# Mask rows inside the key and query tiles of two attentions, a transposed layout for squares, and a copy moved to GpSimd

## What is computed

```
# second: x = layernorm(h)
qkv = x @ qkv_w + qkv_b;  q, k = layernorm(q)*w+b, layernorm(k)*w+b   # over 64
o = softmax(q*scale @ k.T) @ v;  o = gates * o;   h += o @ proj_w + proj_b
# third: x = layernorm(h)
q, k, v = x @ qkv_w.T, in 12 heads of 64
q = q * rsqrt(norm(q, over the 12 heads) + 1e-8);  k likewise
o = softmax(q @ k.T / scale[head]) @ v;   h += o @ w_out.T + b_out
```

## Time and profile before

| | us |
|---|---|
| median of 3 runs | 1608.81 (1606.82 to 1610.09) |
| the profiled execution, its own time | 1603.52 |
| its span, first to last instruction | 1601.7 |

### The profile page before, as it was taken

How to read it: one execution, slowest core, us unless ns; L and a number is a source line. 1 busy time by engine, 2 the same in 40 slices (tenths; PEclk the granted TensorE clock), 3 DMA queues, 4 the chain that set the end, 5 groups by cost and what they waited for, 6 DMA issues and landing times. The chain is left out here.

```text
span 1601.7 us, 27860 instructions
## 1 busy us (share of the span) xinstructions
PE 1283.7 (80%) x9582; PEld 1165.8 (73%) x9582; DVE 1004.0 (63%) x2455; ACT 945.8 (59%) x3313; POOL 454.6 (28%) x447
## 2 busy tenths in 40 slices
PE   1688777777867999999978999999832116999999
PEld 0378767667757898889867999999710116999998
DVE  5663255544547999999847777788575774333333
ACT  2445277777846889889848888888741002222232
POOL 0132001111112333223213233333054003555555
PEclk9688899999978999999989999999955557999999
DMA  5130200020000000000000000000031000000000
GB/s 228 58 114 1 60 1 2 1 60 2 2 1 1 2 2 1 2 1 2 2 1 2 1 2 2 1 2 1 2 88 59 0 0 0 10 1 9 10 9 12
DMA packets 7040, 30.09 MB, mean 19 GB/s; under 512 B 1603, under 2 KB 4400, under 8 KB 5560
## 3 DMA queue, kind: packets, MB, share of 16 engines
q1 hardware_dynamic: 6902, 28.31, 5.5%
HBM read 26.54 MB, written 1.77 MB: 18 GB/s over the span
## 5 line engine op out<-in xcount | busy, mean ns | idle before, releaser
L1101 ACT ACTIVATE t_p<-bank,t_nmax 108x108 f32<-108x108 f32 x792 | 267.3, 355 | 42.1 <-DVE t_nmax L757 40.6
L757 DVE TENSOR_REDUCE t_nmax<-bank 108x4 f32<-108x432 f32 x198 | 119.5, 603 | 145.1 <-PE bank L1267 144.6
L1806 POOL TENSOR_TENSOR f_hid_lo<-f_hid,f_hid_hi 128x432 fp32r<-128x432 f32 (+2 forms) x144 | 145.8, 1014 | 216.0 <-ACT f_hid_hi L1792 216.0
L1267 PEld LDWEIGHTS bank<-t_kT,t_qT 128*108 128x108 f32 x1584 | 187.3, 179 | 2.7
L981 POOL TENSOR_TENSOR t_sq<-t_raw 108x768 f32<-108x768 f32 x88 | 136.2, 1548 | 185.7 <-ACT t_raw L1041 185.3
L1267 PE MATMUL bank<-t_kT,t_qT 128*108 128x108 f32 x1584 | 187.2, 262 | 0.0
L1762 DVE SCALAR_TENSOR_TENSOR f_hid<-bank,f_maskT 128x432 f32<-128x432 f32 (+2 forms) x144 | 80.2, 557 | 166.0 <-PE bank L1689 164.8
L1792 ACT CAST f_hid_hi<-f_hid 128x432 fp32r<-128x432 f32 (+2 forms) x144 | 73.9, 513 | 181.5 <-DVE f_hid L1762 181.4
L1101 ACT ACTIVATION_READ_ACCUMULATOR t_p<-bank,t_nmax 108x1 f32 x792 | 167.0, 211 | 0.0
L775 DVE TENSOR_TENSOR t_p<-t_p,t_rinv 108x432 f32<-108x432 f32 x198 | 149.6, 756 | 6.8
L1276 PE MATMUL bank<-ident,t_p 108*108 108x108 f32 x792 | 109.3, 261 | 31.4 <-ACT t_xt L1031 28.4
(11 more groups left out here) (227 smaller groups left out, 3552.8 us busy)
## 6 DMA issues: line engine op xcount, KB each, us to landing
A_xraw<-in_x SPq DMA_DIRECT2D x4, 2232.6 KB
A_w<-in_tok_w SPq DMA_DIRECT2D x5, 729.0 KB
f_raw_down<-in_w_proj SPq DMA_DIRECT2D x1, 2304.0 KB, 8.5
out_tokens<-h SPq DMA_DIRECT2D x21, 81.0 KB
f_raw<-in_w_mfc SPq DMA_DIRECT2D x1, 1536.0 KB, 7.3
f_raw<-in_w_mfc SPq DMA_DIRECT2D x2, 768.0 KB, 12.2
W_raw<-in_wC SPq DMA_DIRECT2D x1, 1159.0 KB
W_raw<-in_wC SPq DMA_DIRECT2D x2, 579.5 KB
```

Source lines behind the costliest of these rows:

```text
L757: dve.tensor_reduce(b.nmax[:, 4 * c:4 * c + 4], self.sbank[(3 * g + c) % 2][0:GT, 0:4 * GT].rearrange("p (a n) -> p a n", n=GT), AX.X, ALU ...
L1101: act.activation(b.p[g % 2][:, m, :], self.sbank[(3 * g + c) % 2][0:GT, n * GT:(n + 1) * GT], ACT.Exp, bias=b.nmax[:, m:m + 1], accum_out= ...
L1267: mm = pe.matmul(o[0:GT, n * GT:(n + 1) * GT], b.qT[g % 2][:, hd, :], b.kT[g % 2][:, hd // self.per_tile, :], start=False, stop=True, skip ...
L1806: pool.tensor_tensor(self.hid_lo[m % 4][:, c], self.hid[m % 4][:, c], self.hid_hi[m % 4][:, c].bitcast(F32), ALU.subtract).then_inc(s["lo" ...
```

## The change

- **Mask rows.** `kT` becomes one tile for each head (12 instead of 6). In every `qT` and `kT` tile of C and D the half that isn't the head's own now holds three mask rows and otherwise zeroes: one row for each image of the group, 1 for its own tokens in `qT`, -1e30 for all others' in `kT`. The head's matmul so adds the mask itself. The bf16 matmul L1263 is issued only in B, and the heads' matmuls of C and D start their bank themselves. The pads are loaded from DRAM by four DMAs after B; ACT waits for them once, before its first query copy in C. The memset of `qT` in C is gone.
- **Key turns in halves.** With a tile for each head, a key turn is two instructions of 64 partitions: two turns of each group on ACT in C, two on DVE in D.
- **Squares.** In D, POOL writes the squares with the 12 heads innermost (a step of 48 bytes between neighbours), and DVE's sum reads them one behind the other. The bound L741 is gone; ACT's first Ln adds 1e-19 as its bias.
- **Doubled dims.** In C and D DVE's L716 is gone; POOL copies dims 128 to 191 within `xf` (`second`), between the two squares of a round, and PE's transpose of x waits for it (`xd`).
- Two semaphores are merged into others (`wB`, `W_zero2`), and a few waits count accordingly.

```diff
         phase_end(sp, "B")
+        for k in range(2):
+            sp.dma_start(shared.qT[k][:, :, :], ins["q_pads"]).then_inc(loaded["small"], 16)
+            sp.dma_start(shared.kT[k][:, :, :], ins["k_pads"]).then_inc(loaded["small"], 16)
         phase_end(sp, "C")
...
         phase_end(act, "B")
-        C.scalar(act)
+        C.scalar(act, pads=loaded["small"])
...
     b.qT = [plan(f"t_qT{s}", [128, HEADS, GT]) for s in two]
-    b.kT = [plan(f"t_kT{s}", [128, 6, GT]) for s in two]
+    b.kT = [plan(f"t_kT{s}", [128, HEADS, GT]) for s in two]
...
         self.x_tiles = 3 if small else 2
-        self.inits = {"B": 7, "C": 13, "D": 1}[kind]
+        self.inits = {"B": 7, "C": 11, "D": 1}[kind]
...
             dve.tensor_scalar(b.xf[k][:, 0:DIM], x, b.mv[k][:, 0:1], b.rstd[k][:, 0:1],
                               ALU.subtract, ALU.mult).then_inc(s["xf"], 1)
-            dve.tensor_scalar(b.xf[k][:, DIM:256], x[:, 128:DIM], b.mv[k][:, 0:1], b.rstd[k][:, 0:1],
-                              ALU.subtract, ALU.mult).then_inc(s["xf"], 1)
...
             else:
-                dve.tensor_reduce(b.ss[k][:, 64 * m:64 * m + 64], v.rearrange("p (a d) -> p d a", d=64),
+                dve.tensor_reduce(b.ss[k][:, 64 * m:64 * m + 64], v.rearrange("p (d a) -> p d a", a=HEADS),
                                   AX.X, ALU.add).then_inc(s["ss"], 1)
-                after(dve, s["ss"], nth(g, 4, 2 * m))
-
-                dve.tensor_scalar(b.ss[k][:, 64 * m:64 * m + 64], b.ss[k][:, 64 * m:64 * m + 64], 1e-19, None,
-                                  ALU.max).then_inc(s["ss"], 1)
...
             t0 = 3 * (u - 2)
             src = self.turn_bank("qk", g, u)[:, 0:3 * GT].rearrange("p (a n) -> p a n", a=3)
-            dve.tensor_tensor(b.kT[g % 2][:, t0:t0 + 3, :], src,
-                              self.head_scale[:, 6 + t0:9 + t0].unsqueeze(2).to_broadcast([128, 3, GT]),
-                              ALU.mult).then_inc(s["kev"], 1)
+            keys = b.kT[g % 2][:, :, :].rearrange("p (t j) n -> p t j n", j=2)
+            for j in range(2):
+                lo, hi = self.head_rows(j)
+                ins = dve.tensor_tensor(keys[lo:hi, t0:t0 + 3, j, :], src[lo:hi, :, :],
+                                        self.head_scale[lo:hi, 6 + t0:9 + t0].unsqueeze(2).to_broadcast([64, 3, GT]),
+                                        ALU.mult)
+            ins.then_inc(s["kev"], 1)
...
-        if kind != "D":
+        if kind == "B":
             for k in range(2):
                 dve.memset(b.qT[k][:, :, :], 0.0).then_inc(s["init"], 1)
...
         def squares(g, m):
             k = g % 2
             after(pool, s["Qev"], nth(g, self.q_per, 2 * m + 1))
-            if self.kind == "C":
-                after(pool, s["ss"], nth(g - 1, 2, m))
-            else:
-                after(pool, s["ss"], nth(g - 1, 4, 2 * m))
+            after(pool, s["ss"], nth(g - 1, 2, m))
 
             after(pool, s["xl"], nth(min(g + 1, GROUPS - 1), 2, 1))
             v = b.raw[k][:, 768 * m:768 * m + 768]
-            pool.tensor_tensor(b.sq[:, 768 * m:768 * m + 768], v, v, ALU.mult).then_inc(s["sq"], 1)
+            sq = b.sq[:, 768 * m:768 * m + 768]
+            if self.kind == "D":
+
+                v = v.rearrange("p (a d) -> p a d", d=64)
+                sq = sq.rearrange("p (d a) -> p a d", a=HEADS)
+            pool.tensor_tensor(sq, v, v, ALU.mult).then_inc(s["sq"], 1)
...
+        def second(g):
+
+            after(pool, s["xf"], nth(g, 1, 0))
+            after(pool, s["T"], self.turned("x", g - 2))
+            x = b.xf[g % 2]
+            pool.tensor_copy(x[:, DIM:256], x[:, 128:DIM]).then_inc(s["xd"], 1)
+
+        second(0)
+        second(1)
         split_lo(0)
         split_lo(1)
+        after(pool, s["xl"], nth(1, 2, 1))
+        second(2)
         for g in range(-2, GROUPS):
             if g != -2 and g + 3 < GROUPS:
                 split_lo(g + 3)
             if g + 2 < GROUPS:
                 squares(g + 2, 0)
+                if -1 <= g < GROUPS - 4:
+                    second(g + 4)
                 squares(g + 2, 1)
                 add_bias(g + 2)
...
             else:
-                after(act, s["ss"], nth(g, 4, 2 * m + 1))
+                after(act, s["ss"], nth(g, 2, m))
                 sl = slice(64 * m, 64 * m + 64)
 
-                act.activation(b.lg[k][:, sl], b.ss[k][:, sl], ACT.Ln).then_inc(s["norm"], 1)
+                act.activation(b.lg[k][:, sl], b.ss[k][:, sl], ACT.Ln, bias=1e-19).then_inc(s["norm"], 1)
...
+            if pads and g == 0 and u == 0:
+                act.wait_ge(pads, 176)
...
             elif kind == "C":
                 t0 = 3 * (u - 2)
-                ins = act.activation(b.kT[g % 2][:, t0:t0 + 3, :], src, ACT.Identity, scale=self.qk_affine[:, 2:3],
-                                     bias=self.qk_affine[:, 3:4])
+                keys = b.kT[g % 2][:, :, :].rearrange("p (t j) n -> p t j n", j=2)
+                for j in range(2):
+                    lo, hi = self.head_rows(j)
+                    ins = act.activation(keys[lo:hi, t0:t0 + 3, j, :], src[lo:hi, :, :], ACT.Identity,
+                                         scale=self.qk_affine[lo:hi, 2:3], bias=self.qk_affine[lo:hi, 3:4])
...
-            after(pe, s["xf"], nth(g, self.xf_ops, self.xf_ops - 1))
+            after(pe, s["xf"], nth(g, 1, 0))
+            if kind != "B":
+                after(pe, s["xd"], nth(g, 1, 0))
...
-            pe.matmul(o[0:GT, 0:4 * GT], self.owner[:, :], self.other[:, :], start=True, stop=True,
-                      skip_group_check=True)
+            masked = kind != "B"
+            if not masked:
+                pe.matmul(o[0:GT, 0:4 * GT], self.owner[:, :], self.other[:, :], start=True, stop=True,
+                          skip_group_check=True)
             for n in range(4):
                 hd = 4 * c + n
-                mm = pe.matmul(o[0:GT, n * GT:(n + 1) * GT], b.qT[g % 2][:, hd, :], b.kT[g % 2][:, hd // self.per_tile, :],
-                               start=False, stop=True, skip_group_check=True)
+                mm = pe.matmul(o[0:GT, n * GT:(n + 1) * GT], b.qT[g % 2][:, hd, :], b.kT[g % 2][:, hd if masked else hd // 4, :],
+                               start=masked, stop=True, skip_group_check=True)
             mm.then_inc(s["S"], 1)
...
+    q_pads, k_pads = np.zeros((2, 128, HEADS, GT), f)
+    for hd in range(HEADS):
+        at = LO if hd % 2 == 0 else 0
+        own = np.repeat(np.eye(GROUP_IMAGES, dtype=f), TOKENS, 1)
+        q_pads[at:at + GROUP_IMAGES, hd] = own
+        k_pads[at:at + GROUP_IMAGES, hd] = (1 - own) * MASKED
+    A["q_pads"], A["k_pads"] = q_pads, k_pads
```

More of the change, by code:

```diff
@@ L118, in build_in @@
     bank = [ctx.enter_context(nc.psum_tensor(f"bank{i}", [128, 512], F32)) for i in range(8)]
-    loaded = {n: sem("ld_" + n) for n in ("const", "wB", "small", "rawC", "rawD", "tokc", "tokw", "tokx0", "tokx1",
+    loaded = {n: sem("ld_" + n) for n in ("const", "small", "rawC", "rawD", "tokc", "tokw", "tokx0", "tokx1",
                                             "ffn", "rawU", "wdn")}
@@ L150, in _ @@
         pA.load(sp, ins)
-        sp.dma_start(wB[:, :, :, :], ins["wB"]).then_inc(loaded["wB"], 16)
+        sp.dma_start(wB[:, :, :, :], ins["wB"]).then_inc(loaded["small"], 16)
         for dst, name in ((oB[:, :, :], "oB"), (oC[:, :, :], "oC"), (oD[:, :, :], "oD"),
@@ L171, in _ @@
         phase_end(pe, "A")
-        pe.wait_ge(loaded["wB"], 16)
-        pe.wait_ge(loaded["small"], 96)
+        pe.wait_ge(loaded["small"], 112)
         pe.wait_ge(cast_done, 2)
@@ L191, in _ @@
         phase_end(act, "A")
-        act.wait_ge(loaded["small"], 96)
+        act.wait_ge(loaded["small"], 112)
         B.scalar(act, beside=prep.scalar)
         phase_end(act, "B")
-        C.scalar(act)
+        C.scalar(act, pads=loaded["small"])
         phase_end(act, "C")
@@ L212, in _ @@
         phase_end(dve, "A")
-        dve.wait_ge(loaded["wB"], 16)
+        dve.wait_ge(loaded["small"], 112)
         B.vector(dve, beside=prep.vector)
@@ L523, in scalar @@
             act.wait_ge(s_centred, 3)
-            act.wait_ge(s_zero2, 1)
+            act.wait_ge(s_zero, 2)
             act.copy(splitC[3][64:65, :], rawb[64:65, :]).then_inc(s_hi, 1)
@@ L535, in gpsimd @@
         pool.memset(rawb[64:97, :], 0.0).then_inc(s_zero, 1)
-        pool.memset(splitC[3][64:97, :].bitcast(F32), 0.0).then_inc(s_zero2, 1)
+        pool.memset(splitC[3][64:97, :].bitcast(F32), 0.0).then_inc(s_zero, 1)
         pool.wait_ge(s_hi, 1)
-        pool.wait_ge(s_zero2, 1)
+        pool.wait_ge(s_zero, 2)
         pool.tensor_tensor(splitC[1][:, :], raw0[:, :], splitC[0][:, :].bitcast(F32), ALU.subtract).then_inc(s_lo, 1)
@@ L656, in __init__ @@
         self.pv_split = [3] if small else [4, 2]
-        names = ("stats mv log rstd xf T Tev xh xl Q Qev sq ss norm qn S max exp rinv rg pn PV PVev "
```

(20 more changed lines are left out.)

1 line of the change is left out of this document (removed).

## The result

The changed kernel takes 1628.1 us (median of 4 runs, 1623.5 to 1636.0); the kernel before, run beside it, 1607.8 (1605.3 to 1610.1). The ratio is 1.013, 95% interval 1.008 to 1.018: slower by some 21 us. A second set of runs of the same code gave 1.013 again (1.010 to 1.016). The forecast was 1624.3, or +15.5.

A forecast was written before the change was run, and what follows sets the result against it. It took a PE, DVE, ACT ring to bound C and PE alone D. C's rounds +22.7, C's ends -2.4, D's rounds -2.3, D's ends -2.5 sum to +15.5: 1608.8 to 1624.3 us, range 1609 to 1634.

The forecast's parts named there:

- C's key turns: ACT in C: two halved key turns add 1.55 us a round; rounds reach 15.96, +22.7 us over 19 rounds.
- the ring: C after the change: `gate_exp`, next round's root, `normalise`, gate step, `gate_exp` again, 15.96 us a round.
- The mask matmul: PE, three a round at 0.18 us: removal could take C from 14.83 to 14.48, D at most to 13.90.
- two of a round's three mask matmuls lie on its PE part: C's present ring (PE scores, DVE to gate step, ACT's copies of p, PE) would drop from 14.83 to 14.48.
- PE is never late: D's present round: the chain is PE's alone, without idle, 14.43 us.
- to spare: D, chunk 4: PE writes 0.06 us after ACT's chunk 2 copy ends, so PE coming 0.53 earlier would wait.
- rival 1: C: ACT's gap of 1.34 swallows the halves, ring loses only two mask matmuls; total -13.9, 1595 us; chance 0.10.
- Rivals 1, 2 and 4: 2: halves overlap by 93 ns, total +7.4, chance 0.07; 4: ACT's ring met only in part, about -2, chance 0.08.
- D's ring: D through key turn 3, sum, row maximum, ACT, chunk 4: pair +0.62, sum -0.75; round 14.30, -2.3 over 18 rounds.
- Rival 3: D: POOL's strided squares hold DVE up from about 3.5 us each; at 4.4, 1643 us; chance 0.05.
- POOL's copy: Copy of x's doubled dims on POOL: below 0.41 us, nothing taken for it in the total.
- The ends: Starts and tails of phases: C -2.4 (start -2.6, tail +0.2), D -2.5 (start -2, tail -0.5).

The follow-up runs named there:

- gate-first kernel: The changed kernel with DVE's gate step for the next group ahead of `normalise` in C; 1614.3 us, ratio 1.000 to the kernel before.
- lone halves: The kernel before with only D's key turns as two DVE instructions of 64 partitions; 1631.3 us, ratio 1.014, D's rounds 15.60.
- the repeat: The changed kernel run once more, unaltered, as a measure of spread; 1632.5 us, ratio 1.013 to the kernel before.

## Why the prediction was right, and where it wasn't

**C's key turns: right.** A pair is 1.28 to the next instruction, the ring is `gate_exp` to root, `normalise`, gate step, `gate_exp`, and it is 15.96 long as worked out from four rows. The gate-first kernel shows the ring by opening it. Only the first round (14.82) doesn't have it; hence 21.8 and not 22.7.

**The mask matmul: the step failed twice, without harm to the sum.** In C "two of a round's three mask matmuls lie on its PE part" is wrong: the old ring runs over ACT's exps and DVE alone, and PE's gap of 0.34 was a gap beside it. DVE looked packed and PE's copy of p late, and I called that a ring without adding it up; the pieces that do add up to 14.83 are ACT's 10.74 and DVE's 4.09. In D "PE is never late" is wrong by 0.2 a round: the chain gives a wait inside a group as a longer duration of its matmuls. And the 0.06 that PE was said to have "to spare" at chunk 4 was nothing to spare: it is the distance at which PE follows ACT's copy when it waits for it. Neither error showed in the total, since new rings longer than the old ones closed over both. They do show in rival 1: had the halves cost nothing, C would have stayed at 14.83, and by the other terms of the sum the kernel would have gained 7 us, not 14.

**Rivals 1, 2 and 4: out.** Pairs measure 1.28, not 1.07, and they don't hide; the ring is met whole. The 93 ns of overlap that the Trainium skill's page "ScalarE: Activation LUTs", section "What ACT_TABLE_LOAD costs", gives for back-to-back ACTIVATEs don't show here at the border of two halves: two of 0.62 cover 1.25 (641.70 to 642.95, next at 642.98). The rows decide.

**D's ring: right in size, by luck in part.** Forecast 14.30, measured 14.38. The pair's +0.62 holds exactly, the sum's is -0.78 for -0.75, and 0.11 came on top between `normalise` and the row maximum. The base of 14.43 was read from PE's chain; that the ring over DVE and ACT happened to be 14.42 made it a fair base. With 14.42 + 0.62 - 0.78 + 0.11 = 14.37 the working closes. The lone halves' 15.60 shows what the prediction didn't look at: key turn 2 with its sum of 1.5 stood close behind, and only the shorter sums kept it off the path.

**Rival 3, POOL's writes with a step: out.** Squares in D take 1.58 to 1.60 where nothing lengthens them, 1.47 before: +0.12, far from the 3.5 from which it would decide. POOL's copy, put below 0.41, takes 0.23 to 0.24 in a round of D but 0.62 in one of C; giving it back to DVE changes no round, so that cost nothing.

**The ends: mis-sized.** C's head gave 2.9 (forecast 2.6), but its tail lost 2.3 (forecast 0.2): it holds one more full round with both key pairs, 16.10 from `gate_exp` to `gate_exp` (804.60 to 820.70) where it was 14.50 (777.96 to 792.46), and a further pair of key turns behind it. The pads were in time: ACT's first query copy starts 27.8 into C (30.9 before) without a wait for them. D's head gave 1.3 of 2, and its tail, forecast to gain 0.5, lost 1.9 in the profiled execution at a granted clock of 0.95; the repeat's tail, at 1.00 as before, lost 0.3. Together the ends are 3 to 5 over the forecast (the repeat, the profiled execution); with +1.0 to +1.1 from D's rounds and -0.4 to -0.9 from C's that makes +19.2 to +20.5 for C and D out of +15.5, against the 20 to 21 of the medians.

**A's +8 us: most likely not the change.** The 13 profiled executions of this study have A at 185 to 195 (counted from the first instruction), and no edit touches it: before's own code took 193.7 there in the kernel without mask matmuls and 187.2 in the kernel before. B varies as widely, 270.6 to 279.5. The medians leave no room for A's share either, since C and D alone account for them. But A is known only for the profiled executions, and both of the changed kernel lie at the upper end (195.0, 193.7). What sets A's length in a given execution stays open.

## What to carry to other kernels

Before pricing what a removed instruction gives back, close the present ring in numbers: pick an instruction that waits, follow who releases it until you are back at it, and require that the pieces add up to the round. Here it would have shown that the three mask matmuls, the aim of the change, lay on no ring in C, and that in D a ring without them was as long as PE's chain with them. An instruction that was split here for the sake of its destination (two tiles, two halves of partitions) cost its whole time twice, on ACT and on DVE, and in C the wait behind it cost three times what the work added to the round (0.88 and 0.26); reorder what stands between that engine and its answer first.

## What the hardware showed

- Each of two instructions of 64 partitions on different halves lasted as long as one of 128, and they didn't overlap at their border: on ACT it is 1.28 to 1.29 to the next instruction for a pair, against 0.51 to 0.52 for one of 128 partitions (0.62 to 0.66 long, overlapped by its successor), on DVE 1.03 against 0.41.
- DVE's sum of 768 fp32 elements takes 1486 ns with neighbours 64 elements apart and 940 in order; POOL's squares written 48 bytes apart took only 0.12 us more on 1.47.
- In all eight kernels with halved key turns in D the row maximum that follows key turn 3's sum and `normalise` starts 0.97 to 0.99 behind `normalise`, in the four others 0.86 to 0.87 in nearly every round. Why isn't settled.
- DVE's weighing of p (432 columns, two fp32 operands) takes 0.61, but up to 1.9 where a square of POOL starts with it; here from the kernel with the squares' layout alone, whose rounds are nevertheless PE's:

```profile
1016.70 1.60 POOL L978 TENSOR_TENSOR t_sq<-t_raw 108x768 f32<-108x768 f32 x1 [3.23 <-ACT t_raw L1038]
1016.73 1.90 DVE L771 TENSOR_TENSOR t_p<-t_p,t_rinv 108x432 f32<-108x432 f32 x1
...
1020.01 0.61 DVE L771 TENSOR_TENSOR t_p<-t_p,t_rinv 108x432 f32<-108x432 f32 x1
```
